# Second weights split earlier, and 23 unread products for TensorE where attention hands over to the experts

## The reference

```python
x = x + rbf_attention(layernorm(x))                       # softmax over exp(-|q-k|^2)
x = x + cross_attention(ctx, ctx, layernorm(x), mask)     # 16 heads of 16
x = x + moe(layernorm(x))
# moe: gate_logits = xs @ Wg ; top 2 of 8 experts, softmax of the two logits
#      h = relu(xs @ W1[e] + b1[e]) ; out = h @ W2[e] + b2[e] ; weighted sum of the two
```

## Time and profile before

| | |
|---|---|
| median of 3 runs | 589.34 us (588.48 to 590.53) |
| the profiled execution | 592.83 us, of which 590.7 are the span from first to last instruction |
| busy, share of the span | PE 92%, PEld 80%, DVE 66%, ACT 56%, POOL 39% |
| granted TensorE clock, mean | 0.958 of full speed |

### The profile page before, as it was taken

One profiled execution on the slowest core, in us unless ns is written; L12 is line 12 of the kernel. 1 busy time (PEld: TensorE's weight loads), 2 busy tenths in 40 slices (PEclk: granted clock), 3 DMA queues, 4 the chain that ended last, 5 costly groups with the idle time before them and its releaser, 6 DMA issues.

```text
span 590.7 us, 15288 instructions
## 1 busy us (share of the span) xinstructions
PE 546.1 (92%) x5443; PEld 471.2 (80%) x5443; DVE 391.7 (66%) x886; ACT 332.7 (56%) x663; POOL 233.0 (39%) x294
## 2 busy tenths in 40 slices
PE   3978989999999999989979899999999999999991
PEld 2876757787777778654559899999999999999991
DVE  4798776969686886875785689883332456656551
ACT  3763357565756665523554775555556676675650
POOL 6452112323231321210145454435445647664552
PEclk9998899999999999995996899999999999999997
DMA  7788452544528080754047985667787544545432
GB/s 218 203 93 153 62 77 33 100 66 70 94 48 118 21 143 7 111 132 120 23 150 253 321 242 170 181 183 187 205 206 211 126 134 117 153 117 145 107 63 27
DMA packets 56184, 76.63 MB, mean 130 GB/s; under 512 B 6704, under 2 KB 44880, under 8 KB 56112
## 3 DMA queue, kind: packets, MB, share of 16 engines
q1 hardware_dynamic: 46576, 64.28, 43.3%
q0 software_dynamic: 7872, 10.33, 10.5%
q10 hardware_dynamic: 1664, 1.05, 0.6%
HBM read 53.00 MB, written 9.31 MB: 105 GB/s over the span
## 4 chain that ended last, share of the span: by engine, by line
PE 71%; DVE 7%; DMA 7%; ACT 5%; issue 4%; POOL 2%; SPq 1%; POOLq 1%; DVEq 0%; ACTq 0%
PE pair L1436 16%; PE pair L3013 13%; PE pair L3071 10%; PE bank L1436 6%; PE bank L1872 5%; PE pair L1714 5%; PE pair L2898 4%; PE pair L1835 4%; DMA w_now<-L_ffn_W 3%; PE pair L1755 3%; PE pair L1378 1%; DVE row_max L1767 1%; DMA x<-x 1%; DMA slots_in<-xn_rows,gather_now 1%; ACT hid L2866 1%
## 5 line engine op out<-in xcount | busy, mean ns | idle before, releaser
L1767 DVE TENSOR_REDUCE row_max<-pair 128x4 f32<-128x1024 f32 x64 | 77.9, 1221 | 20.9 <-PE pair L1755 19.9
L1852 ACT ACTIVATE exp_ring<-pair 128x1024 f32<-128x1024 f32 x64 | 65.5, 1027 | 33.5 <-PE pair L1835 32.8
L3013 PE MATMUL pair<-slots_t,w_now 128*128 128x128 f32 x672 | 82.7, 284 | 0.0
L3013 PEld LDWEIGHTS pair<-slots_t,w_now 128*128 128x128 f32 x672 | 81.0, 201 | 0.0
L3045 ACT ACTIVATE hid<-pair,b_tile 128x128 f32<-128x128 f32 x168 | 47.8, 366 | 33.8 <-PE pair L3013 33.8
L2966 POOL DMA_INDIRECT out<-y,scatter_now x21 | 35.0, 1665 | 65.7 <-DVE y L3086 53.6
L3021 DVE TENSOR_TENSOR hid_lo<-hid,hid_hi 128x1024 fp32r<-128x1024 f32 x21 | 25.7, 1225 | 45.8 <-ACT hid_hi L3052 45.8
L2771 POOL DMA_INDIRECT out<-y,scatter_now x18 | 32.0, 1778 | 38.9 <-DVE y L3086 33.4
L3071 PE MATMUL pair<-experts_w,hid_hi 128*128 x336 | 44.4, 284 | 0.0
L3071 PEld LDWEIGHTS pair<-experts_w,hid_hi 128*128 128x128 f32 x336 | 40.8, 188 | 0.0
L2898 PE MATMUL pair<-experts_w,hid_hi 128*128 x288 | 40.2, 282 | 0.0
(11 more groups left out here) (348 smaller groups left out, 1447.8 us busy)
## 6 DMA issues: line engine op xcount, KB each, us to landing
w_now<-L_ffn_W SPq DMA_DIRECT2D x21, 1024.0 KB, 5.4
w_now<-L_ffn_W SPq DMA_DIRECT2D x18, 512.0 KB, 3.9
experts_w<-L_ffn_W SPq DMA_DIRECT2D x8, 1024.0 KB, 9.0
k_stack<-ck_hi SPq DMA_DIRECT2D x32, 128.0 KB, 4.3
q_stack<-cq_hi SPq DMA_DIRECT2D x32, 128.0 KB, 4.3
ctx_in<-ctx SPq DMA_DIRECT2D x8, 256.0 KB, 2.8
k_stack<-ck_lo SPq DMA_DIRECT2D x16, 128.0 KB, 5.4
q_stack<-cq_lo SPq DMA_DIRECT2D x16, 128.0 KB, 5.0
```

Source lines behind the costliest of these rows:

```text
L1767: core.e["maxed"].at(eng.tensor_reduce(maxima, pair[:, :].rearrange("p (c t k) -> p c t k", c=KT, t=KT), AX.X, ALU.max))
L1852: core.e["exp"].at(eng.activation(slots.rearrange("p c t q -> p (c t q)"), pair[:, :], ACT.Exp, scale=HD ** -0.5))
L3013: mm = eng.matmul(banks[half][:, f * P:(f + 1) * P], core.w1_now[b.p][:, c, start:start + P], core.slots_t[b.p][:, c, :], start=c == 0, st ...
```

## The change

1. `keep_busy` is new: TensorE multiplies 512 columns of the mask `mask_k` by the identity (both bfloat16) into a bank that nobody reads then. It is called six times in the drain, with 4, 4, 3, 3, 3 and 6 products, 23 in all, three of these behind a wait of their own.
2. The loads of expert 3, 6, 5 and 4 move forward in SP's queue, the last three from the expert iterations into the drain. The split order becomes 0, 1, 2, 3, 7, 6, 5, 4.
3. Splits move forward on ScalarE and VectorE; those of 6, 5 and 4 now stand together in iteration 3. `WATCHED` goes from 8 to 3.
4. VectorE's split of expert 1 now stands ahead of the row sums of batch 6. The normalisations of batches 6 and 7 and the row sums of batch 7 move from around the first rests (`hid_lo`) to behind them.
5. The router products of batches 6 and 7 now stand in the middle of a tile's first product; ScalarE copies the logits of batch 6.
6. Three stores move from ScalarE's queue to SP's.

```diff
-SPLIT_ORDER = (0, 1, 2, 3, 7, 4, 5, 6)
+SPLIT_ORDER = (0, 1, 2, 3, 7, 6, 5, 4)
-WATCHED = 8
+WATCHED = 3
+def keep_busy(core, eng, bank, products):
+    for _ in range(products):
+        eng.matmul(core.psum[bank][:, :], core.ident_bf[:, :], core.mask_k[:, :, :].rearrange("p t k -> p (t k)"),
+                   start=True, stop=True, skip_group_check=True)
 def drain_tensor(core, eng):
     at = drain(core, "tensor", eng)
     last_maximum(at, 0)
+    core.e["hT_lo"].wait(eng, LAST_BATCH.back(3))
+    keep_busy(core, eng, 0, 4)
     at(1, st_maxima)
...
     last_maximum(at, 3)
+    core.e["av_out"].wait(eng, LAST_BATCH.back(2))
+    keep_busy(core, eng, 7, 4)
     last_exponential(at, 1, 0)
     last_maximum(at, 4)
+    keep_busy(core, eng, 7, 3)
     prefix_product(core, eng, 0)
...
     at(0, st_weighted, 3)
+    core.e["exp"].wait(eng, LAST_BATCH, 6)
+    keep_busy(core, eng, 5, 3)
     at(1, st_output)
+    keep_busy(core, eng, 5, 3)
     at(0, st_heads_transposed)
+    keep_busy(core, eng, 5, 6)
 def drain_scalar(core, eng):
...
     split_expert(core, "scalar", eng, 1)
+    split_expert(core, "scalar", eng, 2)
@@ drain_sync
     at(0, st_maxima)
+    core.e["t_tile"].wait(eng, LAST_BATCH.back(1))
+    load_expert(core, eng, 3)
     at(2, st_output)
...
     ex_load(core, "sync", eng, Step(0, 1))
+    core.e["av"].wait(eng, LAST_BATCH)
+    load_expert(core, eng, 6)
+    core.e["p_headsT"].wait(eng, LAST_BATCH)
+    load_expert(core, eng, 5)
     at(1, st_output)
     at(2, st_normalise, 2)
     core.e["p_hT"].wait(eng, LAST_BATCH)
+    load_expert(core, eng, 4)
@@ experts, sync
-        if n in (2, 3, 4):
-            load_expert(core, eng, (4, 5, 6)[n - 2])
+        if n == 2:
+            store_residual(core, eng, LAST_BATCH)
+            store_normalised(core, eng, LAST_BATCH.back(1))
+        elif n == 3:
+            store_normalised(core, eng, LAST_BATCH)
@@ experts, tensor
-        elif n == 4:
-            st_router(core, name, eng, LAST_BATCH.back(1), it)
-        at(2, ex_hidden)
+        if n in (4, 5):
+            ex_hidden(core, name, eng, it.back(2), (0,))
+            st_router(core, name, eng, LAST_BATCH.back(5 - n), it)
+            ex_hidden(core, name, eng, it.back(2), (1,))
+        else:
+            at(2, ex_hidden)
@@ experts, scalar
             st_router_transpose(core, name, eng, LAST_BATCH.back(1), it)
-            store_normalised(core, eng, LAST_BATCH)
-            split_expert(core, name, eng, 7)
+            for x in (6, 5, 4):
+                split_expert(core, name, eng, x)
+            st_router(core, name, eng, LAST_BATCH.back(1), it)
@@ experts, vector
             st_normalise(core, name, eng, LAST_BATCH.back(2), it, 2)
+            split_expert(core, name, eng, 1)
             st_moments(core, name, eng, LAST_BATCH.back(1), it, 2)
             st_transpose(core, name, eng, LAST_BATCH, it, "hT")
-            split_expert(core, name, eng, 1)
...
```

More of the change, by code:

```diff
@@ L1258, in drain_sync @@
     ex_load(core, "sync", eng, Step(0, 0))
-    core.e["t_tile"].wait(eng, LAST_BATCH.back(1))
-    load_expert(core, eng, 3)
     core.e["t_tile"].wait(eng, LAST_BATCH)
@@ L1978, in st_router @@
         core.e["p_gate"].at(mm)
+    elif name == "scalar":
+        core.e["p_gate"].wait(eng, b)
+        core.e["gate"].wait(eng, b.back(1))
+        core.e["gate"].at(eng.activation(core.logits[:, bass.ds(b.v * KT, KT), :],
+                                         ps[:, 0:KT * NE].rearrange("p (t n) -> p t n", t=KT), ACT.Copy))
     elif name == "vector":
         core.e["p_gate"].wait(eng, b)
+        if b.v == NB - 1:
+            core.e["gate"].wait(eng, b.back(1))
         core.e["gate"].at(eng.tensor_copy(core.logits[:, bass.ds(b.v * KT, KT), :],
@@ L2519, in experts @@
         at(3, ex_out)
[L2520 to L2522 removed]
+        if n == 5:
             prefix_product(core, eng, 1)
@@ L2576, in experts @@
         if n == 2:
+            st_best(core, name, eng, LAST_BATCH.back(2), it)
+            st_normalise(core, name, eng, LAST_BATCH.back(1), it, 2)
+            st_moments(core, name, eng, LAST_BATCH, it, 2)
+            split_expert(core, name, eng, 3)
             st_normalise(core, name, eng, LAST_BATCH, it, 2)
-            split_expert(core, name, eng, 3)
+            split_expert(core, name, eng, 7)
+        elif n == 3:
+            for x in (6, 5, 4):
+                split_expert(core, name, eng, x)
         at(3, ex_out)
         if n == 3:
-            st_router(core, name, eng, LAST_BATCH.back(1), it)
             st_best(core, name, eng, LAST_BATCH.back(1), it)
-            split_expert(core, name, eng, 7)
-        elif n == 4:
-            st_router(core, name, eng, LAST_BATCH, it)
-            st_best(core, name, eng, LAST_BATCH, it)
-            routing_choice(core, name, eng, 1)
         elif n == 5:
@@ L3005, in ex_hidden @@
     if name == "tensor":
-        core.w1_in.wait(eng, b)
-        core.m["slots_t"].wait(eng, b)
-        for half in range(2):
+        if 0 in halves:
+            core.w1_in.wait(eng, b)
+            core.m["slots_t"].wait(eng, b)
+        for half in halves:
             core.m["h"].wait(eng, b.back(2), half)
```

31 lines of the change are left out of this document (11 added, 20 removed).

## The result

| | before | after |
|---|---|---|
| median of 19 runs each, side by side | 589.94 us (584.55 to 593.55) | 586.97 us (583.24 to 592.34) |
| ratio to before | | 0.9946, 95% interval 0.9927 to 0.9964 |
| span of the profiled execution | 590.7 us | 585.2 us |
| its mean granted clock | 0.958 | 0.983 |

The account below looks back on a forecast made before the run. TensorE, busy 92% of the span, was taken as the bound, so only its pauses and half-clock stretches could give time. -2.5 + 0 - 3.7 = -6.2 us, from 589.34 to 583.1; own range 580.5 to 586, with rivals 579.5 to 588.

Parts of the forecast that it names:

- Rival 1: Drain: the fillers do not hold the clock and only cost time; 587.2 us, chance 0.22.
- A: Drain to the mask product at 286.17: fillers hold the clock, less 0.9 us uncovered and a new short fall; -2.5 us.
- B: 286.17 to tile 1: uncovered fillers +0.7, shorter half-clock stretch -1.6, wait for third gather +0.9; sum 0 us.
- C: Tile 1 to tile 3: moved router product removes pause and clock fall, -4.0, late splits +0.3; sum -3.7 us.
- Third gather: Before tile 1's product: gather issued beside a split comes 3 to 4 us later, TensorE waits; +0.9 us.
- Early loads and the splits in a row: Tiles 2 and 3: splits in a row on ScalarE and VectorE nearly covered, +0.3 us; early loads had no term.
- Everything else: 0: Logits copy, stores moved to SP, fewer split-table reads on TensorE, and the stretch from 350 us on; 0 us.
- I count +0.3: Tiles 2 and 3: splits in a row and the seventh gather come close to their need; +0.3 us.
- rival 3: SP's queue and DMA rings, 303 to 335: early loads pile up, tile 2's first weights late; 592.6 us, chance 0.08.
- From 350 us on: a plain shift: From 350 us to the end: TensorE has no pause and simply shifts; 0 us.
- Rival 2: Drain and first tiles: the clock stays up throughout; about -10, so 579 us, chance 0.15.

Follow-up runs that it names:

- e1: Kernel after without its 23 fillers and the waits ahead of them; 1.0043 of before, median 591.67 us.
- e2: Kernel before plus the 23 fillers at their places, nothing else; 0.9962 of before.
- e9: Kernel before plus the moved router products of batches 6 and 7, without fillers; 0.9952 of before.
- e8: Kernel before plus the 23 fillers and the moved router products, without ScalarE's copy; 0.9857 of before, median 582.15 us.
- e16: e8 run once more: kernel before plus fillers and moved router products; 0.9876 of before.
- e18: e13 with VectorE's split of expert 1 put back behind batch 6's row sums; 0.9888 of before.
- e13: Kernel after with loads, split order and split places as before, split of expert 1 still ahead of the row sums; 0.9893 of before.
- e6: Kernel after with VectorE's split of expert 1 back behind batch 6's row sums and the copy of batch 7's turned rows; 0.9962 of before.
- e7: Kernel after with the edits of e5 and e6 together; 0.9894 of before from four of six executions, mean of all six 0.9945.
- e14: e11 with SyncE starting its stores ahead of the loads of experts 6 and 5; 0.9937 of before.
- e11: e8 plus the early loads of experts 3, 6, 5 and 4 in the new order, splits one per iteration; 0.9938 of before.
- e4: Kernel after without the last twelve fillers (3, 3 and 6); 0.9997 of before.
- e5: Kernel after with VectorE's splits of experts 6, 5 and 4 spread over iterations 3, 4 and 5; 0.9975 of before.

## Why the prediction was wrong in its size

The direction, the range and most places were right. Rival 1's number, 587.2, is nearest to the measured 586.97, but by luck: its mechanism is refuted by e1 and e2. Point by point, by the terms of the sum:

**Fillers (A, and +0.7 and -1.6 of B): -3.4 forecast, -2.2 measured (e2; with an interval of 0.5 to 4.0 us, which holds 3.4).** In the profiled pair A gave 3.3 us, not 2.5 (5.0, less the 1.6 that were there before it): the clock did not fall behind the maxima, and from the second product of maxima to the mask product it took 5.5 us, not 6.3. And the 17.1 us stretch of the earlier trace rows, from which 4.2 of the gain was taken, was on the long side: e1 and e9 have 6.8 us near there, and 6.9 and 6.8 more some 14 us ahead of it. I carried a gain worked out on an execution at 0.958 to a median of executions at 0.969. That the profiled execution went from 592.83 to 586.97, with 586.6 forecast, is luck again: 1.6 us of it arose before the change. The 3.5 us that I carried over from before did not carry over: the profiled execution of the kernel after is its median.

**Moved router products (C): -4.0 forecast.** Measured -2.8 alone, -6.2 and -5.1 on top of the fillers (e8, e16 against e2). Right in its mechanism, since in e8 pause and half-clock stretch both go, and 1 to 2 us too small on top of the fillers, which makes up for what these lack.

**Third gather: +0.9 forecast.** The wait came, 1.25 us, with the gather issued beside a split as said; its cost to the end is not separable from none (e18 against e13).

**Early loads and the splits in a row: +0.3 forecast, +3.1 measured (the kernel after against e13).** This is the step that failed. Without it the forecast is -6.5, and e13 has -6.3. The words were "Everything else: 0" and, for the blocks, "I count +0.3"; the early loads had no term at all. I had the crowd on SyncE's queue only as rival 3, at 0.08, and looked for it at one customer, tile 2's first weights. In the kernel after these land in time (in e6, e7 and e14, with the same early loads, TensorE does wait 0.84, 0.40 and 1.43 us for them). What comes late in the kernel after is a gather, 7.8 us from its start to the rows' turn and not 5.4, and in e11 a store. The block's price was taken from TensorE's next tile, where the earlier trace rows just cover it, and not from the second routing table behind it, for whose `both` TensorE waits 1.21 us; nor from GpSimd, whose copy in one execution of e4 waits out all of it, though the earlier trace rows showed a copy stretched by one split. How much of the 3.1 us each of these waits makes is open.

**From 350 us on: a plain shift.** So it was in the kernel after: the span behind tile 4's product is 241.6 us before and 241.9 after. In the profiles of e4, e5 and e7 it was not; there the second table's `filler` (0.94, 1.03 and 2.19 us) and in e4 tile 6's rows came late.

**Slips in the working.** Rival 3's terms (3, 1.7, 1 and 1.6, less 2) make 5.3, from which 2 was taken off a second time: its time is 594.6, not 592.6. Rival 2's (-4.2 - 1.6 - 4.0 + 0.3) make -9.5 and 579.8, not 579. TensorE's 16.20 of 17.20 us are 94%, not 95.

Open: how the 3.1 us divide between loads and block (the intervals of e13 and the kernel after overlap by 0.0004), whether the first four fillers help, and why where the clock falls differs from one execution of the same kernel to the next.

## What to carry to other kernels

Where a change bundles fillers, a move and a prefetch, price each against the stretch that it crowds. That nobody waits for a load does not make it free to start it early: look at what is small and urgent behind it in its queue, and at what shares the DMAs with it. A gain taken from half-clock stretches should be taken from the mean clock of many executions, since a single profile can hold a long one. Removing a pause can pay more than the pause where the clock falls behind it: the move of the router products gave 5 to 6 us on top of the fillers, for a pause of 2.85 us.

## What the runs showed of the hardware

- GpSimd beside VectorE's two-input splits can go either way: with the same 0.03 us of lead, an issue took 1.09 us in one execution and 3.31 in another, and a copy that takes 0.19 us elsewhere took 1.26 us or 6.86, the length of three splits.
- SyncE's issue of a 1 MB load took 0.41 us at 298.08 in the kernel after. The next two, right behind another load, took 6.70 us (6.26 in e11), and three in e14 9.59. In the kernel after:

```profile
299.81 6.70 SPq L504 DMA_DIRECT2D experts_w<-L_ffn_W  x2
306.56 3.62 SPq L504 DMA_DIRECT2D out<-x  x1
310.23 0.60 SPq L1373 DMA_DIRECT2D xn_rows<-xn_ffn  x1
```

- 35 executions of the kernel before had mean clocks from 0.954 to 0.978, and the two ends are also the longest and the shortest time, 596.22 and 585.09 us.
- Twenty-three products that nobody reads, about 5 us of work, made two kernels 2.2 and 5.7 us faster.
